# Variance by token in a two-layer conditioned residual kernel: column sums, root and spreading moved between the engines

## What is computed

```python
def _ln(x, g, b):
    m = jnp.mean(x, axis=-1, keepdims=True)
    v = jnp.mean((x - m) ** 2, axis=-1, keepdims=True)
    return (x - m) * jax.lax.rsqrt(v + EPS) * g + b

# layer 0: six normalized or shifted copies of x, weighted, side by side
h = _ln(_ln(x, pw_g[pathway_ids], pw_b[pathway_ids]), cp_g[comp], cp_b[comp])
t, s = _ln(x, tm_g[time], tm_b[time]), _ln(x, ms_g[scale], ms_b[scale])
m, n, r = x + one row per batch from three small networks
w = softmax(aw)
cat = concatenate([w[0]*h, w[1]*t, w[2]*m, w[3]*n, w[4]*r, w[5]*s], axis=-1)
u = silu(cat @ int_W1 + int_b1) @ int_W2 + int_b2
x = x + _ln(u, int_g, int_be)
# layer 1: a modulated product
styles = cond @ (affine_w / 16).T + affine_b
y = einsum(x * styles, weight) * dcoefs
x = x + clip(y + bias, -256, 256)
```

## Time and profile before

| | us |
|---|---|
| Times of the kernel | 1240.94, 1243.15, 1244.84 (median 1243.15) |
| The profiled execution: its own time | 1244.63 |
| its span from first to last instruction | 1242.8 |
| Mean granted clock of TensorE | 0.990 |
| Busy: PE, DVE, ACT, POOL | 1202.5, 946.8, 548.0, 229.0 |

### The profile page before, as it was taken

The page is one execution under the profiler, slowest core; times in us unless marked ns, Lnnn a source line. Parts: engine busy times, 40 slices in busy tenths (PEclk is TensorE's granted clock), DMA queues, the critical chain, the costliest instruction groups (busy, mean ns, idle before and its releaser), DMA issues.

```text
span 1242.8 us, 15227 instructions
## 1 busy us (share of the span) xinstructions
PE 1202.5 (97%) x5268; PEld 948.5 (76%) x5268; DVE 946.8 (76%) x1755; ACT 548.0 (44%) x849; POOL 229.0 (18%) x268
## 2 busy tenths in 40 slices
PE   5899899999999999999999999999999999999996
PEld 4567678878787887878788787887878788787884
DVE  7887877868687796868778687786868779686836
ACT  3545253353634436353443635335353443635352
POOL 3422112102021120212103011210202112021000
PEclk9899899999999999999999999999999999999998
DMA  9931232413223141233314223231322314122001
GB/s 318 363 120 41 68 117 73 129 35 108 78 94 117 39 142 57 87 98 94 110 34 136 63 79 116 74 130 32 112 73 94 117 38 142 57 86 84 26 9 59
DMA packets 52011, 119.50 MB, mean 96 GB/s; under 512 B 6464, under 2 KB 6848, under 8 KB 51840
## 3 DMA queue, kind: packets, MB, share of 16 engines
q1 hardware_dynamic: 36512, 67.58, 17.1%
q0 software_dynamic: 14336, 50.34, 12.5%
q10 hardware_dynamic: 1088, 0.62, 0.2%
HBM read 101.74 MB, written 16.78 MB: 95 GB/s over the span
## 4 chain that ended last, share of the span: by engine, by line
PE 51%; DVE 27%; issue 8%; ACT 6%; DMA 6%; POOL 1%; SPq 1%; DVEq 0%; POOLq 0%; ACTq 0%
PE pre L1152 10%; PE pre L1156 10%; PE pre L1159 9%; DMA gc<-cp_table,k_ids 4%; PE uy L1210 4%; PE uy L1211 4%; PE uy L1213 4%; DVE ug L841 3%; DVE lo_a L848 3%; DVE lo_b L798 3%; PE turn L1131 2%; PE turn L1115 2%; ACT tmp_c L502 2%; DVE raw L714 2%; DVE gb L737 2%
## 5 line engine op out<-in xcount | busy, mean ns | idle before, releaser
L369 POOL DMA_INDIRECT gb<-pw_table,pw_ids x63 | 66.5, 1055 | 368.4 <-PE turn L1115 353.7
L474 ACT ACTIVATE gb<-gb,ra 128x512 f32<-128x512 f32 x63 | 45.7, 726 | 199.3 <-DVE gb L750 197.9
L1210 PE MATMUL uy<-hi_c,w_hi_w 128*128 128x512 f32 x256 | 105.9, 414 | 2.0 <-ACT hi_c L504 1.1
L1213 PE MATMUL uy<-lo_c,w_hi_w 128*128 128x512 f32 x256 | 105.7, 413 | 0.1
L1223 PE MATMUL uy<-hi_a,w_hi_l 128*128 128x512 f32 x256 | 101.2, 395 | 4.7 <-ACT hi_a L532 4.7
L1226 PE MATMUL uy<-lo_a,w_hi_l 128*128 128x512 f32 x256 | 101.4, 396 | 0.7 <-DVE lo_a L848 0.7
L1224 PE MATMUL uy<-hi_a,w_lo_l 128*128 128x512 f32 x256 | 101.0, 395 | 0.0
L1211 PE MATMUL uy<-hi_c,w_lo_w 128*128 128x512 f32 x256 | 100.2, 391 | 0.0
L1190 PE MATMUL pre<-hi_b,w_hi_x 128*128 128x512 f32 x256 | 99.8, 390 | 0.0
L1192 PE MATMUL pre<-lo_b,w_hi_x 128*128 128x512 f32 x256 | 99.6, 389 | 0.0
L1191 PE MATMUL pre<-hi_b,w_lo_x 128*128 128x512 f32 x256 | 99.6, 389 | 0.0
(11 more groups left out here) (218 smaller groups left out, 2903.7 us busy)
## 6 DMA issues: line engine op xcount, KB each, us to landing
xT<-x_turned SPq DMA_DIRECT2D x64, 256.0 KB, 2.9
out_turned<-xT SPq DMA_DIRECT2D x64, 256.0 KB, 2.0
xt<-x_in SPq DMA_DIRECT2D x62, 256.0 KB, 2.7
sel_in<-sel_ids SPq DMA_DIRECT2D x16, 192.0 KB
raw_s<-int_w SPq DMA_DIRECT2D x2, 512.0 KB
raw_h<-int_w SPq DMA_DIRECT2D x1, 1024.0 KB, 23.8
early_hi_w<-mlp_w SPq DMA_DIRECT2D x1, 1024.0 KB, 19.3
raw_w<-mlp_w SPq DMA_DIRECT2D x1, 1024.0 KB, 21.5
```

Source lines behind the costliest of these rows:

```text
L1210: pe.matmul(bank, w_hi["w2"][:, c, cut], hi["c"][:, c, :], start=c == 0, stop=False)
L1213: last = pe.matmul(bank, w_hi["w2"][:, c, cut], lo["c"][:, c, :], start=False, stop=c == C - 1)
```

## The change

All groups now get their variance by token, with tokens on the partitions, as 128x4 values in place of 128x512.

- PE takes four products of one column each: for each block of 128 tokens the weights are the 128x128 piece of `sq0` itself in float32, and the moving operand is the column `vmat`. The result is 128x4: token in the partition, block in the column.
- DVE copies 128x4 out of PSUM (`read_var`), POOL raises it to the power -1/2 in one instruction (`take_root`), DVE multiplies the identity by it to get a 128 x (4 x 128) array with each token's root on its block's diagonal (`spread_root`), and PE spreads that over the partitions by one float32 matmul of 512 columns with the repeated `vmat` as weights. ACT copies this bank into `root` (`read_root`).
- `split_sum`, `low_sum`, ACT's `read_var` and `find_root` go.

```diff
-        uses += [("gs", i, 2), ("h", i, 1), ("gs", i, 3), ("h", i, 2), ("h", i, 3)]
+        uses += [("gs", i, 2), ("h", i, 1), ("gs", i, 3), ("root", i - 1), ("h", i, 2), ("h", i, 3)]
...
+            def take_root(i):
+                pool.wait_ge(var_read, i + 1)
+                nc.gpsimd.tensor_tensor(root_tok[:], var_tok[:], half[:].to_broadcast([P, TPG]), ALU.pow).then_inc(root_taken, 1)
...
                 if more:
                     rstd_x(f)
+                take_root(i - 1)
                 rstd_a(f - 1)
...
-            def split_sum(i):
-                act.wait_ge(sq_added, 3 * i + 3)
-                nc.scalar.activation(sum_r[:, 0, :], sq0[:], ACT.Copy).then_inc(sum_hi, 1)
...
+            def read_root(i):
+                bank = filled(act, "root", i)
+                if i:
+                    act.wait_ge(xq_done, i * C)
+                nc.scalar.activation(root[:], bank, ACT.Copy).then_inc(root_ready, 1)
...
                 split_h(i, 1)
                 split_s(i, 3)
+                read_root(i - 1)
                 split_h(i, 2)
...
+            def read_var(i):
+                bank = filled(dve, "var", i)
+                nc.vector.tensor_copy(var_tok[:], bank[:, 0:TPG]).then_inc(var_read, 1)
+
+            def spread_root(i):
+                dve.wait_ge(root_taken, i + 1)
+                nc.vector.scalar_tensor_tensor(out=root_diag, in0=ident.unsqueeze(1).to_broadcast([P, TPG, P]), scalar=float(D),
+                                               in1=root_tok[:].unsqueeze(2).to_broadcast([P, TPG, P]), op0=ALU.mult,
+                                               op1=ALU.mult).then_inc(diag_ready, 1)
...
-                find_root(i - 1)
+                read_var(i - 1)
                 low_h(i, 1)
+                spread_root(i - 1)
                 make_s(i, 3)
...
             add_square(i, 3)
-            low_sum(i)
+            read_var(i)
             finish(i - 1, 0)
-            find_root(i)
+            spread_root(i)
             finish(i - 1, 1)
             all_x1(i)
...
             def variance(i):
                 bank = fill("var", i)
-                pe.wait_ge(sum_lo, i + 1)
-                pe.matmul(bank, vmat[:, 0:1].to_broadcast([P, P]), sum_r[:, 0, :], start=True, stop=False)
-                pe.matmul(bank, vmat[:, 0:1].to_broadcast([P, P]), sum_r[:, 1, :], start=False, stop=True).then_inc(turn_filled, 1)
+                pe.wait_ge(sq_added, 3 * i + 3)
+                for j in range(TPG):
+                    last = pe.matmul(bank[:, j:j + 1], sq0[:, j * P:(j + 1) * P], vmat[:, 0:1].bitcast(F32), start=True, stop=True)
+                last.then_inc(turn_filled, 1)
+
+            def spread_root(i):
+                bank = fill("root", i)
+                pe.wait_ge(diag_ready, i + 1)
+                pe.matmul(bank, vmat[:, 0:1].bitcast(F32).to_broadcast([P, P]), root_diag.rearrange("p j t -> p (j t)"),
+                          start=True, stop=True).then_inc(turn_filled, 1)
...
                 gain("s", i, 3)
+                spread_root(i - 1)
                 unit_s(i, 1)
...
             unit_y(i - 1, 0)
             variance(i)
-            for o in range(1, C):
+            unit_y(i - 1, 1)
+            spread_root(i)
+            for o in range(2, C):
                 unit_y(i - 1, o)
```

More of the change, by code:

```diff
@@ L43, in bank_uses @@
         uses += [("gt", i, 3), ("gs", i, 0), ("gs", i, 1), ("h", i, 0), ("var", i - 1)]
-        uses += [("gs", i, 2), ("h", i, 1), ("gs", i, 3), ("h", i, 2), ("h", i, 3)]
+        uses += [("gs", i, 2), ("h", i, 1), ("gs", i, 3), ("root", i - 1), ("h", i, 2), ("h", i, 3)]
         if i + 1 < GROUPS:
             uses += [("rows", i + 1)] + [("gt", i + 1, c) for c in range(3)]
-    return uses + [("var", GROUPS - 1)]
+    return uses + [("var", GROUPS - 1), ("root", GROUPS - 1)]
 def build(nc, x, x_turned, sel, idx_pw, idx_k, pw_table, cp_table, mlp_x, mem_w1, noi_res_w1, mlp_w2, mlp_rows, row_src,
@@ L104, in build @@
         vea = sb("vea", [P, 2, 1])
+        var_tok = sb("var_tok", [P, TPG])
+        root_tok = sb("root_tok", [P, TPG])
         ra = sb("ra", [P, 2, 1])
@@ L130, in build @@
         brow, brow_lo = sq12[0:QUAD, 0, :], sq12[0:QUAD, 1, :]
+        root_diag = sq12[:, 1, :].rearrange("p (j t) -> p j t", j=TPG)
         sq = (sq0[:], sq12[:, 0, :], sq12[:, 1, :], sq12[:, 0, :])
@@ L171, in build @@
         v_done, rows_hi, rows_ready, b_used = sem("v_done"), sem("rows_hi"), sem("rows_ready"), sem("b_used")
-        sq_added, sum_hi, sum_lo, var_read, root_step, root_ready = (
-            sem(n) for n in ("sq_added", "sum_hi", "sum_lo", "var_read", "root_step", "root_ready"))
+        sq_added, var_read, root_taken, diag_ready, root_ready = (
+            sem(n) for n in ("sq_added", "var_read", "root_taken", "diag_ready", "root_ready"))
         t_raw, t_hi, t_lo, t_used = sem("t_raw"), sem("t_hi"), sem("t_lo"), sem("t_used")
@@ L215, in last_read @@
                 return h_lo, use[1] * TPG + use[2] + 1
-            if k in ("var", "rows"):
-                return (var_read if k == "var" else v_done), use[1] + 1
+            if k in ("var", "root", "rows"):
+                return {"var": var_read, "root": root_ready, "rows": v_done}[k], use[1] + 1
             return {"mlp_h": (style_ready, 1), "mlp_c": (cT_ready, 3), "batch": (bias_ready, 1),
@@ L455, in _ @@
                     rstd_a(f + 2)
+            take_root(GROUPS - 1)
         @block.scalar
@@ L638, in _ @@
                 split_t(i, 2)
-                split_sum(i - 1)
                 split_t(i, 3)
@@ L643, in _ @@
                 split_h(i, 0)
-                read_var(i - 1)
                 split_s(i, 2)
@@ L681, in _ @@
             u_out(i, 3)
-            split_sum(i)
             y_out(i - 1, 0)
             y_out(i - 1, 1)
-            read_var(i)
+            read_root(i)
             y_out(i - 1, 2)
@@ L811, in add_square @@
                                                    op0=ALU.add, op1=ALU.add).then_inc(sq_added, 1)
-            def low_sum(i):
-                dve.wait_ge(sum_hi, i + 1)
-                nc.vector.tensor_tensor(sum_r[:, 1, :], sq0[:], sum_r[:, 0, :].bitcast(F32), ALU.subtract).then_inc(sum_lo, 1)
+            def read_var(i):
[6 more added lines that the diff above has]
+                                               op1=ALU.mult).then_inc(diag_ready, 1)
             def inverse_root(v, y, h, chain, done):
@@ L825, in inverse_root @@
                 nc.vector.scalar_tensor_tensor(out=y, in0=h, scalar=9.0 / 16.0, in1=y, op0=ALU.add, op1=ALU.mult).then_inc(done, 1)
[L827 to L833, removed]
-                dve.wait_ge(var_read, i + 1)
-                inverse_root(sq[2], root[:], sq0[:], chain, root_ready)
             def make_x1(i, c):
@@ L1028, in _ @@
                 make_s(i, 0)
-                low_sum(i - 1)
                 low_t(i, 3)
```

3 lines of the change are left out of this document (removed).

## The result

The changed kernel took 1254.1 us in the median (1253.53 to 1254.73, four runs), the kernel before, run beside it on the same chip, 1243.3 us (1240.94 to 1244.84): the ratio is 1.0089, with a 95% interval of 1.0071 to 1.0106, so 10.8 us slower. The profiled execution took 1254.73 us with a span of 1252.9, 10.1 us more than the span before.

A forecast was written before the change was run, and what follows sets the result against it. PE, busy 97% of the span, was taken to bound the kernel, with DVE early ahead of `low_h(i, 3)`. Terms 18.9 - 0.6 - 4.5 = +13.8 us on the profiled 1244.63, and so on the median 1243.15, gave 1257.0 us, range 1250 to 1264.

The forecast's parts named there:

- DVE's relief, 0: Passes 2 to 15: DVE gains about 5.1 us a pass, all absorbed in its wait ahead of `low_h(i, 3)`.
- The sign that was to show it: In DVE's timeline, the wait before `low_h(i, 3)` would be 7 us or more.
- PE's work, 1.35 a pass: On PE ahead of `turn_h(i, 3)`: float32 matmuls add 1.6 to 1.9 us, two removed fp32r matmuls save 0.47.
- Rivals B and C: PE's matmuls: B, price doubles or hand-over is late, 1270 us, chance 0.07; C, small products nearly free, 1241.6, chance 0.05.
- 18.9 for the 14 passes: Passes 2 to 15: PE's added 1.35 us a pass shows in full, +18.9 us (16.1 to 20.3).
- The hand-overs, 0.8 us to spare: Root's path PE, DVE, POOL, DVE, PE in pass 7: diagonal ready 0.8 us before PE needs it, cost 0.
- Pass 1, -0.6: PE's standstill before `turn_h(1, 2)` splits into two shorter parts, which may save 2.5 us at half clock; -2.5 to +1.3.
- The other end: Pass 1: DVE's 128x4 copy held up beside POOL's long `w_lo_l` instruction, so the pass ends 1.3 us later.
- The end, -4.5: Last group: remainders 2.7 us earlier, 1.8 us from PE keeping its clock after a 1.7 us standstill; -2.5 to -4.8.
- Rival A: DVE's relief reaches PE and removes the 2.4 us stall at `unit_u` in 14 passes: 1223.4 us, chance 0.07.

The follow-up runs named there:

- fill_ahead: Changed kernel plus six idle DVE instructions of 128x512 just ahead of `low_h(i, 3)` in passes 2 to 15: 1256.7 us, ratio 1.0107 to the kernel before.
- fill_behind: Changed kernel plus six idle DVE instructions of 128x512 just behind `low_h(i, 3)` in passes 2 to 15: 1314.2 us, ratio 1.0577 to the kernel before.
- ends_only: Changed kernel with the new way kept for groups 0 and 15 alone, the old way for groups 1 to 14: 1238.2 us, ratio 0.9963.
- after_move: Changed kernel with three columns' products with the root moved ahead of `low_h(i, 3)` and `finish(i - 1, 0)` moved later: 1223.3 us, ratio 0.9830.
- before_move: Kernel before the change with two columns' products with the root moved ahead of `low_h(i, 3)` and `finish(i - 1, 0)` moved later: 1206.6 us, ratio 0.9708.

## Why the prediction was right

1257.0 was forecast and 1254.1 came, inside the range and on the side given 0.87. By its steps:

- *DVE's relief, 0.* Right, and shown from both sides by `fill_ahead` and `fill_behind`. The sign that was to show it was inexact: the wait before `low_h(i, 3)` is 4.57 us, not over 7, because DVE, being early, also waits 2.14 and 1.01 us at two earlier points. Only the three together make 7.7.
- *PE's work, 1.35 a pass.* Measured 0.90 + 0.87 - 0.47 = 1.30; by the distances of the passes 1.23, and 1.25 with the moved order. The float32 rows of the prologue carried over to 128-wide outputs nearly unchanged. Rivals B and C were both about this size, and both fall with these rows.
- *18.9 for the 14 passes.* Measured 15.0, so 3.9 us less: 0.7 by the size of the price (14 x 0.05), and most of the rest, as far as the traces show, because passes before the change held waits for late `gc` gathers that the changed spacing didn't meet. No run tested that by itself, but in the two kernels with the move, where no gather is late, the full 1.25 a pass shows. The prediction had allowed 2 either way for that.
- *The hand-overs, 0.8 us to spare.* Right: the block is done near 575.2 and PE wants it at 575.97. One piece was mis-sized: POOL's root of 128x4 took 1.02 us, not 0.6 to 0.7.

```profile
572.36 1.02 POOL L394 TENSOR_TENSOR root_tok<-var_tok,half 128x4 f32<-128x4 f32 x1
```

- *Pass 1, -0.6.* In the profiled execution -2.8, a little beyond the low end of -2.5. The reason given for that end is what happened: the standstill came apart in two, and the clock stayed. But it is not assured by the change: the clock stayed in three of the ten traces with the new way in pass 1. In `ends_only` it fell in the same stretch and the gain was 1.2, and in `after_move` and `fill_ahead` it fell for longer and there was none (24.0 us against 23.9). That the profiled execution kept it is luck, and without it the term would have been about 0. The other end, a DVE copy held up by POOL's long instruction, did not occur:

```profile
119.84 0.16 DVE L820 COPY var_tok<-turn 128x4 f32<-128x4 f32 x1
```

POOL's `w_lo_l` ran from 119.68 for 4.58 us over it; the old root's first instruction beside it had taken 4.72. The Trainium skill, SBUF — State Buffer, section Who interferes with whom, says that a DVE instruction with at most one SBUF input, outside the two-port modes, doesn't contend with GpSimd. By that rule the trace agrees, 0.16 us.
- *The end, -4.5.* Measured -2.4. The step that failed is that PE keeps its clock because it stands still for 1.7 us only. The wait came as worked out (1.57), but a second one of 1.02 us for DVE's `lo_a`, which the sum did not have, followed, and the clock fell. Where it was kept, the end took 33.2 us, 4.5 less than the 37.7 before: the other terms of the sum were right.

So the total was good partly by luck, because two errors about the clock, one at either end of the program, cancelled: 2.2 us better in pass 1, 2.1 worse at the end. What is left of the excess, 3.7 us by the profiled executions (13.8 forecast, 10.1 measured), is that of the middle passes.

Rival A had quoted the Trainium skill, Perfetto Trace Analysis, section Optimization Strategies: optimize the engine that blocks the matmul engine. DVE is that engine here, as 60 us in `fill_behind` and -36.6 us in `before_move` show. In these runs the rule holds for the part of its queue behind the last wait that it reaches early; the change worked on the part ahead of it.

## What to carry to other kernels

Before work is taken off an engine that others wait for, look in its own timeline for the last place where it waits before the sequence that is late: what stands ahead of that place is free as long as it fits into the wait, what stands behind it costs its full length here, and moving work across it can give more (36.6 us here, with `finish` moved back in the same edit) than removing it (none). An engine at 97% pays for each small matmul it is given, float32 products of one column included. A path that loses as a whole may still pay where it is latency that counts, as in the last group.

## What the runs showed of the hardware that was not expected

- A float32 product of one column costs as much as one of 32: 8 instructions took 0.81 us here, as they did in the earlier trace rows, and 16 took 1.70.
- POOL's power took 0.56 us in the median on 128x1 in the column power just ahead of the root (0.66 in the other one) and 1.02 on 128x4 (at most 1.13), less than twice as long for four times the values.
- With the same two waits at the end of the program (1.57, then 1.0 us), the granted clock fell to 0.50 for some 6 us in some executions and stayed at 1.00 in others, in traces of kernels that are alike there. It is worth 1.7 to 2.3 us there, and up to 2.8 in pass 1 behind one wait of 3.0 us, and a comparison of two profiled executions can carry it in either direction.
